# Message stage of a two-layer graph kernel: a loop with two slots for its loads, and straight code with three slots and one semaphore for each

## What is computed

```python
h = jnp.maximum(_layernorm(x), 0.0)                # x: result of the attention layer
h = h @ W_in2f
Wij = shifted_softplus(f_ij @ Wf1 + bf1) @ Wf2 + bf2
Wij = Wij * rcut_ij[:, None]
msg = h[idx_j] * Wij                               # idx_j: src, idx_i: dst
agg = jax.ops.segment_sum(msg, idx_i, num_segments=n_atoms)
out = shifted_softplus(agg @ Wo1 + bo1) @ Wo2 + bo2
return x + out
```

## Time and profile before

| | us |
|---|---|
| median of 3 runs | 3317.54 |
| lowest and highest | 3313.77, 3329.19 |
| profiled execution | 3332.83 |
| its span | 3331.0 |
| message stage in it, from the first load to the first load of the output stage's sums | 1797.5 to 2953.4 |

### The profile page before, as it was taken

One profiled execution on the slowest core, in us unless ns is written; L12 is line 12 of the kernel. 1 busy time (PEld: TensorE's weight loads), 2 busy tenths in 40 slices (PEclk: granted clock), 3 DMA queues, 4 the chain that ended last, 5 costly groups with the idle time before them and its releaser, 6 DMA issues. The chain is left out here.

```text
span 3331.0 us, 58371 instructions
## 1 busy us (share of the span) xinstructions
PE 2544.2 (76%) x16674; PEld 1760.3 (53%) x16674; DVE 2454.0 (74%) x6275; ACT 2194.7 (66%) x4803; POOL 1916.5 (58%) x1633
## 2 busy tenths in 40 slices
PE   6776777788887877787886777777777777758887
PEld 5554555444443444444444665666555565547776
DVE  7554555678887877887787778777878778737776
ACT  6655666667777777777775555555555555549998
POOL 2564555267766666766752777777777777720000
PEclk9877899989999999999998889788899899979999
DMA  7665566333333333333333666666666666679998
GB/s 239 241 229 187 212 215 214 118 117 130 127 126 116 130 116 129 118 128 116 124 102 102 117 116 116 115 113 117 119 117 119 116 117 118 114 261 404 424 422 350
DMA packets 323596, 558.99 MB, mean 168 GB/s; under 512 B 135552, under 2 KB 211828, under 8 KB 285794
## 3 DMA queue, kind: packets, MB, share of 16 engines
q1 hardware_dynamic: 226290, 448.50, 40.1%
q0 software_dynamic: 97200, 109.30, 16.6%
HBM read 324.12 MB, written 242.20 MB: 170 GB/s over the span
## 5 line engine op out<-in xcount | busy, mean ns | idle before, releaser
L665 POOL DMA_INDIRECT sum_dram<-b_sum,b_at x392 | 641.1, 1636 | 233.3 <-issue 117.2
L589 POOL DMA_INDIRECT a_xd<-in_x,index x344 | 361.5, 1051 | 162.4 <-issue 100.0
L580 POOL DMA_INDIRECT a_xs<-in_x,index x344 | 364.5, 1060 | 146.8 <-issue 101.6
L598 POOL DMA_INDIRECT x_dram<-a_xo,index x196 | 211.4, 1079 | 290.7 <-DVE a_xo L900 191.7
L1330 PE MATMUL bank<-wl,turned 128*128 128x128 f32 x1568 | 263.8, 319 | 74.4 <-ACT turned L1106 54.4
L802 DVE TENSOR_TENSOR d_x<-bank,d_x 128x512 f32<-128x512 f32 x196 | 134.7, 687 | 239.0 <-remote 142.6
L1330 PEld LDWEIGHTS bank<-wl,turned 128*128 128x128 f32 x1568 | 222.5, 219 | 134.4 <-ACT turned L1106 89.5
L1109 ACT ACTIVATE d_n<-d_x,stat_d_shift,stat_d_rstd 128x128 f32<-128x128 f32 x686 | 283.3, 485 | 0.2 <-DVE stat_d_shift L701 0.2
L1453 PE MATMUL bank<-b_rows,b_same 128*128 128x128 bf16 x4704 | 279.9, 219 | 0.6 <-ACT b_sum L1246 0.6
L1486 PE MATMUL bank<-wo,f_ssp_out 128*128 128x128 f32 x1568 | 225.3, 287 | 55.9 <-DVE f_ssp_out L1055 51.9
L1453 PEld LDWEIGHTS bank<-b_rows,b_same 128*128 128x128 bf16 x4704 | 265.1, 98 | 0.6 <-issue 0.6
(11 more groups left out here) (191 smaller groups left out, 7025.7 us busy)
## 6 DMA issues: line engine op xcount, KB each, us to landing
d_x<-in_x SPq DMA_DIRECT2D x49, 1024.0 KB
x_dram<-d_x SPq DMA_DIRECT2D x49, 1024.0 KB
out<-d_x SPq DMA_DIRECT2D x49, 1024.0 KB, 7.6
sum_dram<-zero SPq DMA_DIRECT2D x48, 1024.0 KB
d_x<-x_dram SPq DMA_DIRECT2D x45, 1024.0 KB, 12.0
d_n<-sum_dram SPq DMA_DIRECT2D x25, 1024.0 KB, 9.1
x_end_dram<-a_xo SPq DMA_DIRECT2D x98, 256.0 KB
b_x<-x_end_dram SPq DMA_DIRECT2D x98, 256.0 KB
```

The lines of the kernel that those rows point to most:

```text
L580: pool.indirect_dma_start(a_xs[t % DEPTH][:, j * F:(j + 1) * F], None, x, column(t, j)).then_inc(gathered[t % GSEM], 16)
L589: pool.indirect_dma_start(a_xd[t % DEPTH][:, j * F:(j + 1) * F], None, x, column(t, TILES + j)).then_inc(gathered[t % GSEM], 16)
L598: pool.indirect_dma_start(x1_dram, column(t, 2 * TILES + j), a_xo[t % 4][:, j * F:(j + 1) * F], None, bounds_check=bound, oob_is_err=False ...
L665: pool.indirect_dma_start(sum_dram, bass.IndirectOffsetOnAxis(ap=b_at[s][:, j:j + 1], axis=0), b_sum[s][:, j * F:(j + 1) * F], None, compu ...
```

## The change

The message stage is written out step by step on all five engines, with no loop. b_x, b_fa, b_goes, b_w and b_src get three slots (DB = 3), and the five loads of a chunk count on one semaphore of their slot, b_ld; whoever reads any of the five waits for all (80 counts a chunk). b_end, sidx and b_col and their loads are gone: the readers take the columns of ends, index and columns where they lie. SP issues the five loads of chunk t together, in the order b_x, b_fa, b_goes, b_w, b_src, after b_y, the transpose of b_fa, b_msg and b_same of chunk t-3 and after the landing of its scatters. The order of the work on the other engines is as before. The memory of four more attention tiles lies ahead of the first tiles that the output stage loads early.

```diff
+DB = 3
@@ the tiles and semaphores
-            b_x = at2("b_x", [P, TILES * F])
+            b_x = [at(f"b_x{i}", [P, TILES * F]) for i in range(DB)]
 ...
-            b_end = at2("b_end", [P, TILES])
-            b_col = at2("b_col", [P, 2 * TILES])
-        a_xd = [sb(f"a_xd{i}", [P, TILES * F]) for i in range(DEPTH - 4 * (PRE - RX))]
+        a_xd = [sb(f"a_xd{i}", [P, TILES * F]) for i in range(DEPTH // 2)]
+        b_ld = sems("b_ld", DB)
+        def loaded(t):
+            return 16 * 5 * (t // DB + 1)
+        def scattered(t):
+            return 16 * sum(TILES - EARLY[1 - u % 2] for u in range(t % DB, t + 1, DB))
@@ SP
-            def load_rows_b(k, u, t0):
 ...
-            def step_b(k, u, t0, ahead=True):
 ...
+            def load_b(t):
+                s = t % DB
+                if t >= DB:
+                    for sent in (b_y_ready, b_fa_turned, b_msg_ready, b_same_ready):
+                        sp.wait_ge(sent, t - DB + 1)
+                        sp.sem_inc(sync_step, 1)
+                    sp.wait_ge(x1_scattered[s], scattered(t - DB))
                     sp.sem_inc(sync_step, 1)
+                c = NC - 1 - t
+                sp.dma_start(b_x[s][:, :], x1_end_dram[c:c + 1, :, :].rearrange("o p f -> (o p) f")).then_inc(b_ld[s], 16)
                 sp.dma_start(b_fa[s][:, :].rearrange("p (j r) -> p j r", j=TILES)[:, :, 0:RBF],
+                             attr_dram[c * C:c * C + C, :].rearrange("(j p) r -> p j r", p=P)).then_inc(b_ld[s], 16)
+                sp.dma_start(b_goes[s][:, :], goes_dram[c:c + 1, :].broadcast_to([P, C])).then_inc(b_ld[s], 16)
+                sp.dma_start(b_w[s][:, :], weight_dram[c:c + 1, :].broadcast_to([P, C])).then_inc(b_ld[s], 16)
+                sp.dma_start(b_src[s][:, :], src_dram[c:c + 1, :].broadcast_to([P, C])).then_inc(b_ld[s], 16)
+            for t in range(NC):
+                load_b(t)
@@ POOL
-                pool.wait_ge(sidx_ld[s], 16 * turn(k, u))
-                pool.wait_ge(b_x_ld[s], 32 * turn(k, u))
+                pool.wait_ge(b_ld[t % DB], loaded(t))
 ...
+                    pool.indirect_dma_start(x1_dram, column(NC - 1 - t, 2 * TILES + j),
@@ DVE
-                dve.wait_ge(b_x_ld[s], 32 * turn(k, u))
+                dve.wait_ge(b_ld[t % DB], loaded(t))
 ...
-                    dve.wait_ge(b_goes_ld[o], 16 * turn(k, u - 1))
-                    dve.wait_ge(b_w_ld[o], 16 * turn(k, u - 1))
-                    dve.wait_ge(b_src_ld[o], 16 * turn(k, u - 1))
-                    dve.wait_ge(b_col_ld[o], 16 * turn(k, u - 1))
 ...
+            for t in range(NC + 2):
+                step_b(t // 2, t % 2, t, ahead=t + 1 < NC, front=t < NC, mid=1 <= t <= NC, back=t >= 2)
@@ PE
-                    pe.wait_ge(b_fa_ld[s], 16 * turn(k, u))
+                    pe.wait_ge(b_ld[t % DB], loaded(t))
```

More of the change, by code:

```diff
@@ L202, in at2 @@
                 return [at(f"{name}{i}", shape, dt) for i in range(2)]
-            b_x = at2("b_x", [P, TILES * F])
[L205 to L208, removed]
+            b_x = [at(f"b_x{i}", [P, TILES * F]) for i in range(DB)]
+            b_fa = [at(f"b_fa{i}", [P, TILES * 32]) for i in range(DB)]
+            b_goes = [at(f"b_goes{i}", [P, C], BF16) for i in range(DB)]
+            b_w = [at(f"b_w{i}", [P, C]) for i in range(DB)]
+            b_src = [at(f"b_src{i}", [P, C]) for i in range(DB)]
             b_y = at2("b_y", [P, TILES * F])
@@ L470, in load_sums @@
+            for t in range(NC):
+                load_b(t)
+            for t in range(NC - DB, NC):
+                sp.wait_ge(x1_scattered[t % DB], scattered(t))
             def load_sums(g, slot):
@@ L666, in adds @@
                                             b_sum[s][:, j * F:(j + 1) * F], None, compute_op=ALU.add).then_inc(added[s], 16)
[L668 to L675, removed]
+            for t in range(NC):
+                scatters(t // 2, t % 2)
+                if t >= 2:
+                    adds(t // 2, t % 2 - 2, first=t == 2)
             for u in range(2):
@@ L948, in _ @@
                 dve.wait_ge(early_scattered[s], 16 * EARLY[s] * HALF)
[L949 removed]
+            for i in range(DB):
                 padded = b_fa[i][:, :].rearrange("p (j r) -> p j r", j=TILES)
@@ L1022, in step_b @@
                     for j in range(TILES):
-                        last = dve.tensor_scalar(b_same[o][:, j, :], b_src[o][:, :], b_col[o][:, j:j + 1], None, ALU.is_equal)
+                        last = dve.tensor_scalar(b_same[o][:, j, :], b_src[c][:, :], columns[:, 8 * (NC - t) + j:8 * (NC - t) + j + 1], None, ALU.is_equal)
                     last.then_inc(b_same_ready, 1)
@@ L1037, in _ @@
             mask_b(0, 0)
[L1038 to L1042, removed]
-            step_b(HALF - 1, 0, 4)
-            step_b(HALF - 1, 1, 5, ahead=False)
-            step_b(HALF, 0, 4, ahead=False, front=False)
-            step_b(HALF, 1, 5, ahead=False, front=False, mid=False)
+            for t in range(NC + 2):
+                step_b(t // 2, t % 2, t, ahead=t + 1 < NC, front=t < NC, mid=1 <= t <= NC, back=t >= 2)
             def f_ssp(c, q, c0):
@@ L1252, in _ @@
             norms_b(0, 0, 0)
-            for u in range(4):
-                step_b(0, u, u, mid=u >= 1, back=u >= 2)
-            with act.Fori(2, HALF - 1) as k:
-                for u in range(2):
-                    step_b(k, u, 4 + u)
-            step_b(HALF - 1, 0, 4)
-            step_b(HALF - 1, 1, 5, ahead=False)
-            step_b(HALF, 0, 4, ahead=False, front=False)
-            step_b(HALF, 1, 5, ahead=False, front=False, mid=False)
+            for t in range(NC + 2):
+                step_b(t // 2, t % 2, t, ahead=t + 1 < NC, front=t < NC, mid=1 <= t <= NC, back=t >= 2)
             def f_abs_of(c, q):
@@ L1464, in _ @@
             pe.wait_ge(load_weight, 16 * (2 + 2 * TILES))
-            for u in range(4):
-                step_b(0, u, u, mid=u >= 1, back=u >= 2)
-            with pe.Fori(2, HALF) as k:
-                for u in range(2):
-                    step_b(k, u, 4 + u)
-            step_b(HALF, 0, 4, front=False)
-            step_b(HALF, 1, 5, front=False, mid=False)
+            for t in range(NC + 2):
+                step_b(t // 2, t % 2, t, front=t < NC, mid=1 <= t <= NC, back=t >= 2)
             def f_turn(c, q, slot, m, c0):
```

57 lines of the change are left out of this document (14 added, 43 removed).

## The result

| | before | after |
|---|---|---|
| median, us | 3323.4 (4 runs) | 3526.0 (4 runs) |
| ratio, 95% interval | | 1.0609 (1.0571 to 1.0647) |
| span of the profiled execution | 3331.0 | 3522.2 |
| b_y of the first and of the last chunk | 1800.5, 2897.9 | 1800.6, 3088.0 |
| chunk of the message stage, from these | 11.31 | 13.27 |

The change makes the kernel 6% slower, about 200 us; 105 were forecast. The whole of it lies between the first and the last b_y: (13.27 - 11.31) x 97 = 190 us of the 191 us between the spans. The stages before and behind it have not moved: 1800.5 and 1800.6 us up to the first b_y, 433 and 434 us behind the last.

The account below looks back on a forecast made before the run. The prediction took a loop through b_y, b_same's release and the five loads to set the chunk: 5.8 + 0.3 + 6.4 = 12.5 us. Over 95 chunks, plus 3 at the start, +105 us gave 3422, range 3320 to 3500.

Parts of the forecast that it names:

- What bounds the kernel before: Message stage, 11.43 us a chunk: DVE waits 1.92 us for b_y's loads; floors 9.51 us (DVE) and 10.53 (POOL).
- Part 1: SP's loads: the last release is b_same of chunk t-3, not the scatter, 3.65 us before the data are wanted.
- First term: Message stage, from b_y's start to b_same's end on DVE: taken as 5.8 us of the chunk time.
- Part 2: The five loads: b_y waits for the last, b_src, though it needs b_x alone; 5.25 to 7.75 us, taken as 6.4.
- third term: Message stage, from the first load's issue to b_y's start: taken as 6.4 us of the chunk time.
- The high end: First issue to b_y if the engines serve all SP's loads and three adds in one go: 7.75 us.
- rival 3: Message stage: queues collide fully and code fetches fall among the loads; 13.1 to 13.85 us a chunk, 3480 to 3550; 12 in 100.
- Part 3: Columns in place: b_x in perhaps 0.5 us sooner, a gain swallowed because b_y waits for b_src.
- Part 4: Message stage without loops: code fetches and saved branches taken as 0, up to 0.3 us a chunk as the dear end.
- Start: b_y of chunk 0 waits for five loads instead of two and starts about 3 us later.
- Rival 1: Message stage: each load lands as a lone one does, 5.25 us; chunk 11.35 us, 3313 us in all; 13 in 100.
- Rival 2: Message stage faster: release early enough, DVE's wait shrinks, POOL bounds at 10.53 us a chunk; 3232 us; 10 in 100.

Follow-up runs that it names:

- e9: The changed kernel with b_x on its own semaphore and each load released by its own reader; ratio to the kernel before 0.9843, chunk 10.59 us.
- e12: As e9, with three instead of two of a chunk's four scatters sent in the attention stage; ratio to the kernel before 1.0082, chunk 10.09 us.
- e6: The changed kernel with a fourth slot for b_src alone, the five loads still in one train; ratio to the kernel before 0.9872, chunk 10.69 us.
- e2: The changed kernel with SP waiting before each load only for that tile's reader, one semaphore kept; ratio to the kernel before 0.9872, chunk 10.71 us.
- e1: The changed kernel with b_x on its own semaphore, b_y and the scatters waiting for it alone; ratio to the kernel before 0.9915, chunk 10.84 us.
- e3: The changed kernel without the four adds of each chunk to the table of sums; ratio to the kernel before 1.0460, chunk 12.79 us.
- e11: The changed kernel with b_w's load cut to 16 rows after the first three chunks; one run, 3097.5 us, chunk 12.04 us.
- e8: The changed kernel unaltered, measured again; 3520.5 us against 3322.4 for the kernel before, chunk 13.26 us.
- e4: The kernel before in straight code, without the three small loads, columns read in place; ratio to the kernel before 0.9886, chunk 10.99 us.

## Why the prediction was wrong

The direction and the mechanism were right, the size was not, and the time lies above the range. By its steps:

- **What bounds the kernel before.** Right in the main. With the train out of the way the chunk is 10.6 to 10.8 us, near POOL's floor of 10.5 and not at DVE's 9.5. That floor is not POOL's work alone, though: it has 9.98 us of its own in e9, and e12 reaches 10.09 with 8.5.
- **Part 1, what releases a load.** Right: SP waits for b_same in each chunk, never for the scatter. First term 5.58 us for 5.8, second 0.26 for 0.3. The tests are e6 and e2, which move the release.
- **Part 2, the last load ends the wait.** Right: e1 changes only who waits for which load, and the wait is gone.
- **Part 2, the size of the third term.** This is the step that failed: the time from the first issue to b_y was put at 6.4 us and measured 7.57. The sum took the train at the start of the stage for the nearest row and wrote "1.05 + 4.6 + 0.35 = 6.0", as if the 4.6 us from b_goes's issue to the end did not depend on what runs ahead. There b_x had left 2.36 us ahead of b_goes; in the new order it leaves 0.85 ahead (2312.14, 2312.99), and its data and b_fa's 512 pieces are still being moved: over the turns of the trace the pieces of 80 bytes move from 1.9 to 2.6 us behind b_x's issue, and those of b_goes behind them. I allowed 0.4 us for this and the adds together. The adds alone are 0.5 (e3), and the train without them takes 7.07 where the sum had 6.0. The high end, 7.75, came within 0.2 us, but in part by luck: it serves the five loads and three adds one after the other, and without the adds it would give 1.0 + 4.06 + 0.35 = 5.4 us, where e3 measures 7.07. It priced a load at the time that its pieces keep the engines busy, 4.06 us for the five (3.8 in the kernel after; the three small copies had a share in the 4.06), and e11 measures 1.3 for one of three equal loads. Why a load costs that much in a train, no run shows. The issues themselves took less than the sum had, 1.87 us from b_x to b_src for 2.05.
- **The range.** Its upper end, 3500, was cut from a bound of 13.85 us a chunk, and 13.27, or 13.41 in the steady part, lies inside that bound. The time was rival 3's (3480 to 3550, 12 in 100), for partly the wrong reason: adds do fall on the train, 0.5 us, but no part of fetches shows. In the kernel after, 10 of 86 trains have a 16 KB piece of code moving in their first 6 us, and they take 7.67 us on the mean for 7.53 of the others; in e8 it is 7.47 (9 of 87) for 7.54, with an uncertainty of 0.1 to 0.2. The range should have gone to the bound.
- **Part 3, columns in place.** The 0.5 us by which b_x would be in use sooner measured 0.42 (e4). That it is swallowed in the change was not measured by itself; it follows from b_y's wait for b_src.
- **Part 4, straight code.** Taken as 0; it is a gain of 0.24%. The page's instruction queue went from 40 to 103 pieces (0.66 to 1.69 MB), and no wait of the loop is put down to them. The Trainium skill's sentence that kernels prefer unrolling (Runtime: NRT & Kernel Launch, "Instruction fetch mechanics") has the right sign here, at 0.1 us a chunk; that a taken branch is what costs it is not shown.
- **Start.** The 3 us are there, but do not show: the first b_y comes 6.45 us behind SP's first issue (1794.15) for 2.97 before, while SP issues 3.4 us earlier than in the kernel before, and b_y stands at 1800.6 for 1800.5.
- **Sum.** 97 x (7.57 - 6.4) = 113 us, less the 0.26 us a chunk of the first two terms, is some 88 us, and 190 - 105 = 85 us is what the forecast fell short of in the stage.
- **Rival 1** fell: a load in the train does not land like a lone one (7.57 for 5.25). The Trainium skill's fit of a fixed 2.0 us plus bytes over 436 GB/s is given for one DMA on GpSimd's path (DMA: Bandwidth & Descriptors, "Anatomy of one DMA — SWDGE (gpsimd) path"). Carried over to SP's last load it makes an estimate of 4.65 us; 7.57 were measured, so it is no price for these loads sent back to back. **Rival 2**, with POOL near its bound, happened in e1, e2, e6 and e9, by other edits than this one.

## What to carry over

The depth of a ring of buffers is what the latest of its releases leaves of it. Three slots that are refilled together after the last reader of the old data gave these loads 3.7 us, where they need over 7. Such bunching also leaves the DMA engines 0.86 busy in one half of the chunk and 0.21 in the other, which a mean of 0.52 hides. Wait for the load that is read, not for the train; and price a load in a train by what a train takes, not by its lone landing or by its bytes. Of a change of several parts, measure each alone: here two of three were gains, and with the third mended (e9) all of it gave 1.6%.

## What was not expected of the hardware

- A 256 KB load in the middle of five holds the last back by 1.3 us (7.57 to 6.26 with one eighth of b_w's pieces, 16 of 128), while SP's DMAs of a chunk keep the 16 engines busy for 28.3% of 13.41, 3.8 us, in a train of some 6 us from its first bytes. Without the adds the engines are busy 0.66 of the train's time (e3), and still it takes 7.07 us.
- The kernel before takes 3323 us on the chip of the result and 3322 on that of e8, but 3005 and 3004 on two others, 10% less. No profile of it was taken on the faster ones, but the other kernels (e12 apart, which changes the attention stage) have their first b_y at 1485 to 1494 us there, for 1790 to 1810 on the slower ones: some 310 of the 318 us lie ahead of the message stage.
- The first add of a chunk takes 2.55 us in the kernel after and the next 1.57; the mean over all adds was 1.64 before, and 1.80 over the first ones. The first starts now while DVE makes the third part and b_before:

```profile
2311.81 2.55 POOL L639 DMA_INDIRECT sum_dram<-b_sum,b_at  x1 [2.06 <-ACT b_sum L1207]
2314.67 1.57 POOL L639 DMA_INDIRECT sum_dram<-b_sum,b_at  x1 [0.31 <-issue]
...
2311.89 0.68 DVE L994 TENSOR_TENSOR b_rows<-b_rest,b_rows 128x512 bf16<-128x512 f32 x1
2312.50 0.42 DVE L1001 TENSOR_TENSOR b_before<-b_same,lower 128x512 bf16<-128x512 bf16 x1
```

That the one causes the other was not tried; POOL has 2 us to spare there, so it costs nothing.
